# A graph layer's last stage: TensorE adds the residual row in every tile, GpSimd only gathers

## The reference

```python
        m = v * attn[..., None]
        out = jax.ops.segment_sum(m, dst, num_segments=n).reshape(n, H * D)
        out = out @ Wo.T + bo
        out = node_feat + out
        mean = out.mean(axis=0)
        var = jnp.mean(jnp.square(out - mean), axis=0)
        out = (out - mean) * jax.lax.rsqrt(var + EPS) * gamma + beta
        return out
    ...
    x = _layernorm(x + _L1_gnn_ref(x, edge_attr_512, src, dst, ...), axis=-1)
```

## Time and profile before

| | us |
|---|---|
| median of 3 runs | 1469.31 |
| lowest and highest | 1468.95, 1478.6 |
| the profiled execution's own time | 1476.03 |
| its span (first to last instruction) | 1474.3 |
| first product of the last stage's tile loop, from the span's start | 1325.18 |

### The profile page before, as it was taken

One profiled execution on the slowest core, in us unless ns is written; L12 is line 12 of the kernel. 1 busy time (PEld: TensorE's weight loads), 2 busy tenths in 40 slices (PEclk: granted clock), 3 DMA queues, 4 the chain that ended last, 5 costly groups with the idle time before them and its releaser, 6 DMA issues. The chain is left out here.

```text
span 1474.3 us, 25107 instructions
## 1 busy us (share of the span) xinstructions
PE 1340.4 (91%) x7880; PEld 1134.9 (77%) x7880; DVE 1091.8 (74%) x2016; ACT 605.1 (41%) x1127; POOL 831.4 (56%) x808
## 2 busy tenths in 40 slices
PE   1698888699999994999999999999999999959997
PEld 1588888588777873999999999999999999744443
DVE  5345544588888871387888888888888888877887
ACT  1356555255555552232232222332222333155786
POOL 2655552466666653355555555555555554567885
PEclk9899999899999996999999999999999999969999
DMA  3577764666666645144444444444444443749955
GB/s 121 158 237 262 252 210 165 207 214 221 220 221 217 219 156 172 30 130 129 130 130 130 131 135 134 136 134 140 130 139 133 146 146 110 236 169 355 309 196 188
DMA packets 122537, 257.91 MB, mean 175 GB/s; under 512 B 20819, under 2 KB 21267, under 8 KB 122354
## 3 DMA queue, kind: packets, MB, share of 16 engines
q1 hardware_dynamic: 92018, 175.83, 36.9%
q0 software_dynamic: 29920, 80.38, 17.8%
q10 hardware_dynamic: 544, 1.05, 0.2%
HBM read 197.18 MB, written 73.60 MB: 184 GB/s over the span
## 5 line engine op out<-in xcount | busy, mean ns | idle before, releaser
L174 PE MATMUL pse<-w_lo,w_hi 128*128 128x256 f32 (+1 forms) x1440 | 465.0, 323 | 5.8 <-DVE w_lo L1227 4.4
L175 PE MATMUL pse<-w_hi,w_lo 128*128 128x256 f32 (+1 forms) x1440 | 460.6, 320 | 0.0
L176 PE MATMUL pse<-w_hi 128*128 128x256 f32 (+1 forms) x1440 | 460.5, 320 | 0.0
L174 PEld LDWEIGHTS pse<-w_lo,w_hi 128*128 128x128 f32 x1440 | 276.0, 192 | 27.5 <-DVE w_lo L1227 5.9
L176 PEld LDWEIGHTS pse<-w_hi 128*128 128x128 f32 x1440 | 275.8, 192 | 19.7
L175 PEld LDWEIGHTS pse<-w_hi,w_lo 128*128 128x128 f32 x1440 | 276.2, 192 | 18.3
L711 POOL TENSOR_TENSOR node_y<-node_z,node_x 128x512 f32<-128x512 f32 x79 | 102.0, 1291 | 100.4 <-issue 80.0
L1011 POOL TENSOR_TENSOR acc_x<-acc_x,node_rows 128x512 f32<-128x512 f32 x72 | 115.4, 1603 | 49.4 <-DMA node_rows<-x_table 45.2
L174 PE MATMUL psn<-w_lo,agg_hi 128*128 128x512 f32 x316 | 125.3, 396 | 0.0
L176 PE MATMUL psn<-w_hi,agg_hi 128*128 128x512 f32 x316 | 125.2, 396 | 0.0
L175 PE MATMUL psn<-w_hi,agg_lo 128*128 128x512 f32 x316 | 125.1, 396 | 0.0
(11 more groups left out here) (257 smaller groups left out, 2905.8 us busy)
## 6 DMA issues: line engine op xcount, KB each, us to landing
node_x<-in_x SPq DMA_DIRECT2D x79, 256.0 KB
x_table<-node_x SPq DMA_DIRECT2D x79, 256.0 KB, 2.0
node_rows<-x_table SPq DMA_DIRECT2D x79, 256.0 KB
coef_all<-coef_table SPq DMA_DIRECT2D x38, 512.0 KB
edge_part<-part SPq DMA_DIRECT2D x20, 512.0 KB
sum_table<-sums SPq DMA_DIRECT2D x40, 256.0 KB
part_in<-edge_part SPq DMA_DIRECT2D x20, 512.0 KB
out_dram<-rows_over_w_lo SPq DMA_DIRECT2D x40, 256.0 KB
```

The costliest lines, as they stand in the source:

```text
L174: pe.matmul(to, left[0], right[1], start=first, stop=False)
L175: pe.matmul(to, left[1], right[0], start=False, stop=False)
L176: return pe.matmul(to, left[0], right[0], start=False, stop=last)
```

## The change

TensorE adds x1 through the identity in every tile. `by_pool`, its count `pool_adds`, the semaphore `add_ok`, GpSimd's adds and their lag `ADD` are gone. GpSimd's list is 79 gathers. A gather for tile k waits for the copy of tile k as before, and for the sum of tile k - 8 where it waited for the scaling of tile k - 8. Nothing else is changed.

```diff
-                for k in range(NT + ADD):
-                    if k < NT:
-                        pool.wait_ge(u_ok, k + 1)
-                        wait(pool, us_ok, k - R + 1)
-                        nc.gpsimd.indirect_dma_start(out=u(k), out_offset=None, in_=g.msg_table,
-                                                     in_offset=bass.IndirectOffsetOnAxis(ap=g.last_edge[:, k:k + 1], axis=0),
-                                                     bounds_check=EP - 1, oob_is_err=False).then_inc(u_in[k % R], 16)
-                    j = k - ADD
-                    if j >= 0 and by_pool(j):
-                        pool.wait_ge(us_ok, j + 1)
-                        nc.gpsimd.tensor_tensor(u(j), u(j), x1(j), ALU.add).then_inc(add_ok, 1)
+                for k in range(NT):
+                    pool.wait_ge(u_ok, k + 1)
+                    wait(pool, sum_ok, k - R + 1)
+                    nc.gpsimd.indirect_dma_start(out=u(k), out_offset=None, in_=g.msg_table,
+                                                 in_offset=bass.IndirectOffsetOnAxis(ap=g.last_edge[:, k:k + 1], axis=0),
+                                                 bounds_check=EP - 1, oob_is_err=False).then_inc(u_in[k % R], 16)
...
                     wait(pe, norm_ok, j - 6)
                     pe.matmul(bank(j), ones_r[:], shift[:].rearrange("p k n -> p (k n)"), start=True, stop=False)
-                    if by_pool(j):
-                        pe.wait_ge(add_ok, pool_adds(j))
-                    else:
-                        pe.wait_ge(u_ok, j + 1)
-                        pe.matmul(bank(j), g.ident[:], x1(j), start=False, stop=False)
-                        pe.wait_ge(us_ok, j + 1)
+                    pe.wait_ge(u_ok, j + 1)
+                    pe.matmul(bank(j), g.ident[:], x1(j), start=False, stop=False)
+                    pe.wait_ge(us_ok, j + 1)
                     pe.matmul(bank(j), g.ident[:], u(j), start=False, stop=True).then_inc(sum_ok, 1)
```

More of the change, by code:

```diff
@@ L1532, in finish_stage @@
     PAIR, NORM = 10, 12
-    ADD = 4
     with ExitStack() as ctx:
@@ L1572, in bank @@
             return sum_banks[j % 7][:]
[L1574 to L1578, removed]
         const_in = g.const_in
@@ L1589, in finish_stage @@
         u_before = [landed(NT - 1 - s, 0, 0, 4) for s in range(4)] + [landed(ET - 1 - s, 0, 0, 4) for s in range(4)]
-        us_ok, add_ok, sum_ok, stat_ok, root_ok, scale_ok, norm_ok = (sem(n) for n in (
-            "fin_u_scaled", "fin_u_and_x_added", "fin_y_summed", "fin_stat", "fin_root_ok", "fin_scale_ok", "fin_norm"))
+        us_ok, sum_ok, stat_ok, root_ok, scale_ok, norm_ok = (sem(n) for n in (
+            "fin_u_scaled", "fin_y_summed", "fin_stat", "fin_root_ok", "fin_scale_ok", "fin_norm"))
         y_out = [sem(f"fin_out{s}") for s in range(4)] + g.row_out + g.u_out
```

## The result

The changed kernel takes 1486.36 us (median of 7 runs, 1484.21 to 1492.19), the kernel before 1472.67 us beside it (7 runs, 1468.95 to 1478.6). The ratio is 1.0092, 95% interval 1.0072 to 1.0111: slower by 0.9%, about 13.5 us (0.0092 x 1472.67). The profiled execution took 1484.21 us with a span of 1482.5.

What follows compares the result with a forecast made beforehand. GpSimd's list was taken as the second half's pace, with late gathers added in the first. TensorE gains 25.8 us, less 12.75 of waits: +13.1 on the median 1469.31 gives 1482.4, rounded to 1483; range 1478 to 1489.

Steps and rivals of the forecast that it cites:

- What bounds the kernel before: Edited stage: GpSimd's list sets the second half's pace at 1.746 us per tile; late gathers add in the first half.
- The price of the products: TensorE's queue: 30 tiles each gain two f32 passes of 0.86 us, 25.8 us more.
- All waits go: TensorE's present waits in the stage, 12.75 us, all vanish, so the stage grows by 13.05 us.
- the time to spare: Between a gather's issue and TensorE needing its bank: 2.5 us left at the worst latency seen.
- the 0.65 of the prediction: GpSimd's expected idle time per tile after the change, 0.65 us, a sign of the forecast.
- Start, tail, the wait, the ports: Stage's start unchanged, tail still 6.85 us, GpSimd's new wait free, scalings gain little from the adds' removal.
- A: First-half stalls are absent in an ordinary run, so the change costs 17 us: 1486; chance 0.18.
- B: Stalls survive as gather latency grows beyond the 2.5 us to spare: 4 to 6 us, 1486 to 1488; chance 0.16.
- C: TensorE's 0.43 us between passes shrinks without GpSimd's adds: 1454 us; chance 0.04 together with D.
- D: TensorE has hidden slack; stage falls to VectorE's 1.51 us per tile, 21 less: 1448; chance 0.04 with C.
- a rounding for stalls: Total raised from 1482.4 to 1483 us, since the slower profiled run may hold extra stalls in this stage.
- the remaining stalls: Stalls left in the stage after the change: costed at zero, bounds 0 and 4.0 us.

Runs made afterwards that it cites:

- second profile: Kernel before, no edit, profiled a second time: 1475.53 us, with 69.60 us for tiles 1 to 36.
- 2 of 8: Kernel before with GpSimd adding x1 in 2 tiles of 8 (j % 8 in 1, 5): ratio 0.9995 to the kernel before.
- 5 of 16: Kernel before with GpSimd adding x1 in 5 tiles of 16 (1, 4, 7, 10, 13): ratio 0.9985 to the kernel before.
- 3 of 8: The kernel before itself, GpSimd adding x1 where j % 8 is 1, 4 or 6: ratio 1, median 1472.67 us beside the changed kernel.
- 1 of 8: Kernel before with GpSimd adding x1 in 1 tile of 8 (j % 8 = 4): ratio 1.0037 to the kernel before.
- 4 of 8: Kernel before with GpSimd adding x1 in 4 tiles of 8 (odd j): ratio 1.0037 to the kernel before.

## Why the prediction was right

**What bounds the kernel before.** Held. GpSimd's list is the pace of the second half: without its adds the half falls to 68.47 us, TensorE's own work, and with a fourth add in eight it rises to 78.49 against 79.2 worked out. Busy shares would have named TensorE, which has 97% in that half.

**The price of the products.** 30 x 0.86 = 25.8 us by 1.95 per tile. Measured 1.953 per tile, so 152.3 for 78 tiles where 152.1 was worked out, and 152.95 as cut, since the last stretch reaches to VectorE's start. By halves +3.5 and +10.4 where +3.4 and +9.7 stood.

**All waits go.** Held: PE has no idle row from tile 1 on. But the time to spare was smaller than the 2.5 us of the prediction. It let the gather start about 0.7 us after the sum of tile k - 8; in the changed kernel it starts 2.06 us after TensorE's first product of tile k - 7 (1406.81 against 1404.75 above, for tile 50), since the copy starts 0.65 us after that product, takes 0.62, and the gather starts 0.8 us after the copy's end. TensorE begins tile 50 at 1418.42, 11.6 us after its gather, so 11.6 - 10.4 = 1.2 us are to spare. These were not used up even with adds put back before the gathers. VectorE's wait for gathers shrank to 2.0 us and did not reach PE. GpSimd idles 0.96 us per tile: the 0.65 of the prediction, and the pause of 0.30 that stands behind a gather in the earlier trace rows too. The clock's drop of the earlier trace rows is gone (granted 1.00 against 0.97 in the first half).

**Start, tail, the wait, the ports.** The tail is 6.83 against 6.85, the old wait gives the same stage, the scalings take 659 ns as before. The scaling reads one input from PSUM, so the rule of the Trainium skill (GPSIMD Engine Reference, section 8, Key points) on VectorE instructions with two SBUF inputs is not tested by it; the scalings' mean shows no contention with or without adds. The prediction's "By it VectorE would become quicker" does not follow from that rule for an instruction with one SBUF input.

**The rivals.** A (no stalls in an ordinary run) has the second profile against it, 69.60 us in the first half, and the timed runs: their difference has an interval of 10.6 to 16.3 us, and A says 17. B (stalls survive) falls: no idle time on PE from tile 1 on in four profiles of kernels in which TensorE adds in every tile. C and D (products cheaper than 0.86, or overlapped) fall with 1.953 in every tile.

**The number.** 1483 was 1469.31 + 13.1 and a rounding for stalls. The difference came to 13.5 to 13.7; what moved was the kernel before itself, whose median over seven runs is 1472.67. With it the forecast would have read 1486. The measured 1486.36 is, as a bare number, what A (1486) and B (1486 to 1488) gave, and 3.4 us over the forecast; only the profiles and the difference of the two kernels tell that the forecast's mechanism is the one that holds. The reason that was given for the rounding, that the profile of before may have had unusual stalls in this stage, found no support: the second profile had more.

**What the prediction missed.** It named no cause for the late gathers and looked only at the mean rate of the DMA engines. It put the remaining stalls at zero for the right reason, the slack, but the stalls follow the single large loads.

## What to carry to other kernels

Where two engines share one kind of work by turns, write down what a tile costs each list, idle time between instructions included, and compare lists, not busy shares: GpSimd's gathers cost 1.00 us busy but 1.30 in its queue. The best share lies near the point where the lists are equal: here 2 of 8, 5 of 16 and 3 of 8 are within 0.15% of one another, 1 of 8 and 4 of 8 cost 0.4%, and moving all the work to TensorE 0.9%. To tell which transfer a stall belongs to, move the transfer: here the stalls' period followed the loads' period, though the mean share of the DMA engines had fallen.

## What the runs showed of the hardware

In the kernel before with its loads spread, five stalls of its first half each began 4.2 to 4.8 us after a load of 1 MB from HBM was issued, with the DMA engines at 0.90 on average; I had expected the mean share to decide. On GpSimd a gather is busy for 1.00 us and the next one starts 1.30 us after it; a 128x512 add between two gathers moves the second by 1.17 us, though it is busy for 1.28. An add on GpSimd of rows with themselves, into other rows, takes 1.05 us where one of two different inputs, into one of them, takes 1.28.
